# Fewer 32x32 blocks written for the inversion, and the turned inverse blocks fetched before the plain ones

## What is computed

```python
mixed = jax.nn.silu(_causal_conv1d(hidden_states @ w_qkv, conv_w))
q, k, v = split(mixed);  q, k = _l2norm(q), _l2norm(k)
def step(St, inp):                       # for every one of 256 tokens
    St = St * jnp.exp(g_t)[..., None, None]
    v_old = jnp.einsum('bhk,bhkv->bhv', k_t, St)
    delta = (v_t - v_old) * b_t[..., None]
    St = St + k_t[..., None] * delta[:, :, None, :]
    o = jnp.einsum('bhk,bhkv->bhv', q_t, St)
core = core * rsqrt(mean(core * core) + EPS) * norm_weight * silu(z)
return core @ w_out
```

## Time and profile before

| | us |
|---|---|
| median of 3 runs | 1287.56 (1286.76 to 1291.09) |
| the profiled execution | 1299.38 |
| its span | 1297.6 |
| PE busy | 1114.2 (86%) |
| DVE busy | 840.6 (65%) |
| POOL busy | 653.1 (50%) |
| ACT busy | 648.8 (50%) |

### The profile page before, as it was taken

One profiled execution on the slowest core, in us unless ns is written; L12 is line 12 of the kernel. 1 busy time (PEld: TensorE's weight loads), 2 busy tenths in 40 slices (PEclk: granted clock), 3 DMA queues, 4 the chain that ended last, 5 costly groups with the idle time before them and its releaser, 6 DMA issues.

```text
span 1297.6 us, 22128 instructions
## 1 busy us (share of the span) xinstructions
PE 1114.2 (86%) x8190; PEld 840.1 (65%) x8190; DVE 840.6 (65%) x1469; ACT 648.8 (50%) x1192; POOL 653.1 (50%) x1076
## 2 busy tenths in 40 slices
PE   4899999855898989899799979897998999698747
PEld 3676666523576776768486757676775768486636
DVE  5532222278776788587959776886879497758304
ACT  3321222144574657376556747573756476466412
POOL 2601000158384838574774758385838555682720
PEclk8989999987897999899989989997999899899959
DMA  9720110231313140413131331303140313212011
GB/s 326 319 96 24 42 45 21 94 103 68 67 59 100 37 127 8 128 32 103 35 99 36 98 84 50 101 33 102 53 113 24 110 32 103 45 64 42 19 31 41
DMA packets 140761, 101.06 MB, mean 78 GB/s; under 512 B 113904, under 2 KB 127856, under 8 KB 137328
## 3 DMA queue, kind: packets, MB, share of 16 engines
q1 hardware_dynamic: 139120, 95.45, 24.8%
q0 software_dynamic: 1536, 4.20, 0.9%
HBM read 75.57 MB, written 24.05 MB: 77 GB/s over the span
## 4 chain that ended last, share of the span: by engine, by line
PE 50%; DVE 23%; issue 5%; ACT 2%; DVEq 0%
DVE conv L1104 7%; DVE nm L1141 7%; PE rv L1369 6%; PE pj L1236 5%; PE ra L1336 5%; PE pj L1237 4%; PE pj L1238 4%; PE rv L1352 4%; DVE eg L1113 4%; PE ra L1326 3%; PE ra L1319 3%; PE rv L1344 2%; PE rv L1353 2%; PE pk L1277 2%; DVE acc L1210 2%
## 5 line engine op out<-in xcount | busy, mean ns | idle before, releaser
L1104 DVE SCALAR_TENSOR_TENSOR conv<-pj,taps,conv 128x510 f32<-128x510 f32 (+2 forms) x384 | 285.2, 744 | 93.3 <-ACT conv L997 82.8
L960 POOL TENSOR_TENSOR halves<-halves 64x30 f32<-64x30 f32 (+14 forms) x480 | 262.8, 547 | 37.6
L957 POOL TENSOR_TENSOR halves<-halves 64x30 f32<-64x30 f32 (+14 forms) x480 | 249.8, 520 | 37.6
L1236 PE MATMUL pj<-xhi,whi 128*128 128x512 f32 x384 | 184.1, 479 | 58.5 <-DVE conv L1104 55.4
L1238 PE MATMUL pj<-xhi,wlo 128*128 128x512 f32 x384 | 158.7, 413 | 0.0
L1237 PE MATMUL pj<-xlo,whi 128*128 128x512 f32 x384 | 158.6, 413 | 0.0
L1369 PE MATMUL rv<-wo,gated 128*128 128x256 f32 x512 | 152.7, 427 | 1.7 <-DVE acc L1210 1.4
L1141 DVE SCALAR_TENSOR_TENSOR nm<-pk,wneg,eg 128x512 f32<-128x512 f32 (+1 forms) x256 | 139.5, 606 | 14.5 <-PE pk L1280 14.4
L1236 PEld LDWEIGHTS pj<-xhi,whi 128*128 128x128 f32 x384 | 76.2, 198 | 111.7 <-DVE conv L1104 67.4
L997 ACT ACTIVATE conv<-pj,taps 128x512 f32<-128x512 f32 x128 | 87.6, 685 | 108.4 <-PE pj L1238 107.6
L951 POOL MEMSET halves<- 64x32 f32 x16 | 2.4, 152 | 273.0 <-DMA halves<-n_scratch 273.0
(11 more groups left out here) (197 smaller groups left out, 2210.8 us busy)
## 6 DMA issues: line engine op xcount, KB each, us to landing
eg<-eg_scratch SPq DMA_DIRECT2D x16, 1536.0 KB
wraw<-w_heads SPq DMA_DIRECT2D x16, 776.0 KB
w1a<-w_up SPq DMA_DIRECT2D x10, 1024.0 KB, 6.9
n_scratch<-nm SPq DMA_DIRECT2D x64, 96.0 KB, 2.8
w2a<-w_down SPq DMA_DIRECT2D x8, 512.0 KB
wo<-w_out SPq DMA_DIRECT2D x16, 256.0 KB
halves<-n_scratch SPq DMA_DIRECT2D x32, 128.0 KB, 2.5
r_scratch<-halves SPq DMA_DIRECT2D x32, 128.0 KB
```

The costliest lines, as they stand in the source:

```text
L957: gp.tensor_tensor(tmp, rb[:, 0:t, t:t + 1].to_broadcast([4 * NM, t, w]), rb[:, t:t + 1, t + 1:].to_broadcast([4 * NM, t, w]), ALU.mult).t ...
L960: gp.tensor_tensor(rb[:, 0:t, t + 1:], rb[:, 0:t, t + 1:], tmp, ALU.add).then_inc(elim, 1)
L1104: v.scalar_tensor_tensor(out=y, in0=it.pbank[item][:, :, 0:S - s], scalar=taps[par][:, piece(j)[0], KS - 1 - s:KS - s], in1=y, op0=ALU.mul ...
L1236: te.matmul(bank, whi[par][w], xhi[:, k, cols], start=(k == 0), stop=False)
```

## The change

Three edits in the functions of SP and one wait on POOL:

- `blocks_out` writes only runs 0 and 1 of the three. A DMA takes one run, so there are 8 DMAs of 32 x 8 pieces of 128 bytes, where there were 4 of 32 x 24. `n_scratch` is laid out so that the load of `rb` reads one contiguous area.
- The load of `rb` is one DMA of 64 partitions where it was two of 32; POOL's wait counts 16 a group instead of 32.
- In `blocks_back` the three loads of the turned blocks come before the four of the plain ones. The wait for `a_full` moves with them, and the wait for `r_out` stands now behind them.

```diff
-    n_dram = nc.dram_tensor("n_scratch", (4, REP * B * 3, C32, C32), F32).ap()
+    n_dram = nc.dram_tensor("n_scratch", (2, 4, REP * B, C32, C32), F32).ap()
@@ blocks_out
                     for q in range(4):
                         first = C32 * q
-                        cols = nm[par][first:first + C32].rearrange("p m w e -> p (m w e)").rearrange("p (k s) -> p k s", s=S)
-                        sp.dma_start(n_dram[q].rearrange("k i x -> i k x"), cols[:, :, first:first + C32]
-                                     ).then_inc(blocks_out_sem, 16)
-                    at_least(sp, blocks_out_sem, 64, n, 64)
+                        cols = nm[par][first:first + C32].rearrange("p m w e -> p (m w e)").rearrange("p (m k s) -> p k m s", k=3, s=S)
+                        for k in range(2):
+                            sp.dma_start(n_dram[k, q].rearrange("m i x -> i m x"), cols[:, k, :, first:first + C32]
+                                         ).then_inc(blocks_out_sem, 16)
+                    at_least(sp, blocks_out_sem, 128, n, 128)
                     at_least(sp, r_out, 32, n, 0)
-                    for c in range(2):
-                        sp.dma_start(rb[2 * NM * c:2 * NM * (c + 1)],
-                                     n_dram.rearrange("q (m k) i x -> k q m (i x)", k=3)[c]).then_inc(rb_in, 16)
+                    sp.dma_start(rb.rearrange("p i c -> p (i c)"), n_dram.rearrange("k q m i x -> (k q m) (i x)")).then_inc(rb_in, 16)
@@ blocks_back
+                    sp.wait_ge(rt_out, 32 * n + 32)
+                    at_least(sp, a_full, 1, it.a_before("U2_1"), 0)
+                    for q, tile in enumerate((t64[0:C32, :, 0:C32], t64[C32:C64, :, C32:C64], tc2[C64:C64 + C32])):
+                        sp.dma_start(tile, rt_dram[q].rearrange("m i c -> i m c")).then_inc(turned_in, 16)
                     sp.wait_ge(r_out, 32 * n + 32)
-                    at_least(sp, a_full, 1, it.a_before("U2_1"), 0)
                     for q in range(4):
                         rows = slice(C32 * q, C32 * (q + 1))
                         src = r_dram[q].rearrange("m i c -> i m c")
                         sp.dma_start(rf[rows, :, C32 * q:C32 * (q + 1)], src).then_inc(back_in, 16)
-                    sp.wait_ge(rt_out, 32 * n + 32)
-                    for q, tile in enumerate((t64[0:C32, :, 0:C32], t64[C32:C64, :, C32:C64], tc2[C64:C64 + C32])):
-                        sp.dma_start(tile, rt_dram[q].rearrange("m i c -> i m c")).then_inc(turned_in, 16)
@@ eliminate
-                    gp.wait_ge(rb_in, 32 * n + 32)
+                    gp.wait_ge(rb_in, 16 * n + 16)
```

## The result

| | before | after |
|---|---|---|
| median, us (four runs each) | 1289.32 (1286.76 to 1294.43) | 1307.55 (1305.81 to 1311.14) |
| profiled execution, us | 1299.38 | 1305.81 |
| its span, us | 1297.6 | 1304.1 |

The changed kernel is slower: ratio 1.0141 (1.0117 to 1.0166), 18.2 us by the medians. Forecast were +8.0 us and a range up to 1302.0, so the sign was right and the size was not: the time lies beyond the upper end.

A forecast was written before the change was run, and what follows sets the result against it. Bound: the path from `nm` to LA1 of odd groups, counted 8 times. Terms +1.5 - 0.2 - 0.3 = +1.0 us a group, +8.0 us in all, 1295.6 us on the median of 1287.6; range 1285 to 1302.

The forecast's parts named there:

- What bounds it: LA1 of odd groups waits on PE for the turned inverse blocks; the path from `nm` to LA1 counts 8 times.
- The way out, +1.5: SP's block writes, four issues become eight: `rb` loaded after 5.8 us instead of 4.26, +1.5 us; bounds +0.8 and +2.1.
- Rival 4: SP's queue fills: eight issues meet the longest issue once in each odd group, 1.5 us more, +20 us, 1307.6; chance 0.06.
- One load of `rb`, -0.2: Load of `rb` before POOL: one DMA saves the second issue but carries both halves' bytes; -0.2 us, between nothing and 0.5 saved.
- Turned first, -0.3: Loads on SP: without the four `rf` loads ahead, the turned writes land a little earlier; -0.3 us, between 0 and 0.7.
- The plain blocks behind them: Four plain loads after the turned ones: LA2 does not need them earlier; 0, with 1.3 us of cover.
- The rest of a pair: From LA1 of an odd group to the next odd group's blocks leaving: 65.5 us, beside 54.9 of path, 120.4 per two groups.
- 2.6 us of slack: Even groups: the last turned load lands 2.6 us before LA1 starts in group 4, the smallest slack; charged 0.
- a sign against me: The prediction is wrong if PE's wait in even groups appears.
- the terms did not cancel: Rival: an issue costs 0.42 and turned loads gain all 0.7 us; -0.1 a group, -1 us, 1286.8; chance 0.20.
- later issues are not short: Rival: 303 ns of a first issue holds for all eight writes; -0.4 a group, -3.2 us, 1284.4; chance 0.07.
- Rival 3: The pieces decide: the way out falls by the third of pieces; -1.3 a group, -10 us in sum, 1277.2; chance 0.05.

The follow-up runs named there:

- `pad2`: Kernel before plus two idle memsets on POOL behind the wait for `rb`, ahead of every inversion; median 1315.99 us, ratio 1.0109.
- `after_again`: The changed kernel run and profiled once more, nothing altered; median 1317.69 us, ratio 1.0158 to the kernel before.
- `swap_only`: Kernel before with only the turned loads moved ahead of the plain ones; median 1299.91 us, ratio 0.9995.
- `nolo`: Kernel before and changed kernel, each with POOL's `wlo` subtract cut to 8 of 768 columns from group 2 on; ratios 0.9980 and 1.0079 to the kernel before.
- `split8`: Kernel before with its four writes a group cut into eight DMAs of 32x12 pieces, all pieces still written; median 1317.71 us, ratio 1.0121.

## Why the prediction was wrong in size

- **What bounds it: right.** PE waits for the turned blocks in odd groups only, the path from `nm` to LA1 counts eight times, and `pad2` fits that with 1.07 us of time for one of measured path, though its interval would also hold a higher price.
- **The way out, +1.5: right by luck.** Measured +1.42 in the mean (+1.12 in `after_again`). But an issue takes 0.45, not the 0.49 taken from `rf`, and lands after 1.7, not 2.2: undisturbed it was +0.77, my lower bound of 0.8. The other 0.65 comes with the packets that I had not looked at. Rival 4, which had a 2 us issue once in each odd group, rested on the longest issue of the earlier trace rows, which has such a packet beside it, and landed at 1307.6 where 1307.55 was measured. That is luck too: it blamed the filling of SP's queue and charged 1.5 us a group, and what is shown is 0.65 a group and two other terms.
- **One load of `rb`, -0.2: wrong, the step that failed on the path.** Measured +0.33 in the mean and +0.65 between the medians (+0.57 in the mean of `after_again`). I bounded it by 0 and 0.5 saved and took no loss into the range, though the sentence itself said that the landing would grow with twice the data.
- **Turned first, -0.3: half of it.** From the turned write to the first turned load it is 5.12 us in the mean of the odd groups against 5.27: -0.15. The plain blocks behind them cost nothing that `swap_only` could tell.
- **The sum**: 1.42 + 0.33 - 0.14 from POOL's copy to LA1, and -0.07 in POOL's inversion, make 1.55 us a group, 12.4 for eight, against 8.0.
- **The rest of a pair is 65.5 us whatever the change does: wrong, the other step that failed.** It grew by 5.9 us in seven pairs. The cause is scans that meet POOL's subtract: they are 6.2 us longer in these stretches, and in the `nolo` pair, where they can't meet, the growth is 0.6. The even groups were held safe with 2.6 us of slack: LA1 now waits 1.09 us in group 4 (way out 8.03 us, with two packets in it) and 0.61 in group 0, which was named as a sign against me and did appear.
- **The other rivals** fell: the terms did not cancel, later issues are not short (0.45 against the first one's 0.30 us), and the pieces do not decide (0.32 us of the undisturbed way out, by `split8`). Rival 3 rested on the sentence of the Trainium skill, "DMA: Bandwidth & Descriptors", section "Issuing engines are not separate DMA queues", that initiating a DMA is usually short beside the DMA itself; the trace does not agree, with 3.76 us of issues in a way out of 5.03.

## What to carry to other kernels

Where a small round trip through DRAM lies on the critical path, count its DMA issues and what stands between the last producer and the last issue: writing early what is ready gave 0.7%, writing less in more DMAs lost 1.4%. A step taken from an undisturbed row is a floor, so take the mean over all groups, and ask what else uses its DMA engines. And when one engine's work moves by a microsecond or three, look for long GpSimd instructions with operands in SBUF that now start just ahead of a VectorE one with two SBUF inputs. The stage ahead of the groups took 275 to 291 us from one execution to the next, so traces are better compared from a common event than by their spans.

## What was not expected of the hardware

- A pair of scans on DVE takes 1.42 us alone and 4.49 us when POOL's 3.45 us subtract begins 0.09 us ahead of it.
- Instruction packets of 16 KB go with held issues in a row of small DMAs: one issue of 1.68 us instead of 0.45, and a way out of 6.07 us in the mean instead of 5.03.
- A load of 256 KB on 64 partitions landed in 3.5 us, two of half the bytes in 2.4 each, with 0.37 us of issue between them: two are through 0.5 to 0.7 us sooner.
- PE ran at a granted clock of 0.50, 1.2 GHz, for some 10 to 14 us around and after each wait at LA1 of the odd groups (41 us with the one of group 15), in sum for 177 us of the groups against 157 before. Wait by wait the length does not decide: in before 5.23 us had 13.7 us at the lower level with it and 6.37 us had 10.2. What these us cost was not measured by themselves.
